# A two-layer cross-attention kernel: the last stage's weight halves are made in the feed-forward and loaded during attention 1

## The reference, cut to what matters

```python
x = x + L0_xattn(layernorm(x), ctx)            # int8 fake-quantised projections
x = x + L0_ffn(layernorm(x))                   # 512 -> 2048 -> 512, gelu of a rounded hidden state
x = x + L1_xattn(layernorm(x), ctx, mask)      # ends as below
x = x + L1_ffn(layernorm(x))

# end of L1_xattn
delta = rs * (ctx_heads @ Wo.T + bo)
delta = (delta - mean(delta)) / sqrt(var(delta) + 1e-5) * gamma + beta

# L1_ffn: a shared two-layer part, and one expert weighted by the softmax over the top 2 gates
logits = x @ W_gate.T
shared = relu(x @ W_up.T) @ W_down.T
out = shared + sum(softmax(top_2(logits))) * (x @ W_expert)
```

## Time and profile before

| what | value |
|---|---|
| three runs: median (lowest to highest) | 2832.75 us (2831.48 to 2833.82) |
| profiled execution: time, and span from first to last instruction | 2833.96 us, 2832.1 us |
| TensorE: matrix products busy | 2595.5 us, 92% of the span |
| VectorE, ScalarE, GpSimd busy | 64%, 44%, 43% |
| mean granted TensorE clock | 0.968 of full speed |
| transfers | 383.83 MB, mean 136 GB/s |
| last stage, 2558 to 2832: TensorE busy | 208.77 of 274.10 us |

### The profile page before, as it was taken

The page is one execution under the profiler, slowest core; times in us unless marked ns, Lnnn a source line. Parts: engine busy times, 40 slices in busy tenths (PEclk is TensorE's granted clock), DMA queues, the critical chain, the costliest instruction groups (busy, mean ns, idle before and its releaser), DMA issues. The chain is left out here.

```text
span 2832.1 us, 35427 instructions
## 1 busy us (share of the span) xinstructions
PE 2595.5 (92%) x14009; PEld 1677.5 (59%) x14024; DVE 1806.8 (64%) x2532; ACT 1249.2 (44%) x1876; POOL 1220.5 (43%) x312
## 2 busy tenths in 40 slices
PE   8999899998999999999958999997999999992998
PEld 7888788985444444445426777775344433432776
DVE  4553444466666766667525755544999999985664
ACT  3221212313656665656632222222888877872211
POOL 1000000004999999999930000000777777772110
PEclk9999999999999999999988999998999999996999
DMA  8676666565534435253044333336977777703110
GB/s 297 205 253 226 221 227 236 188 199 121 104 81 89 97 72 113 62 119 65 16 150 170 112 103 122 110 103 165 197 153 153 154 154 153 154 21 119 61 44 30
DMA packets 206071, 383.83 MB, mean 136 GB/s; under 512 B 16104, under 2 KB 91912, under 8 KB 205840
## 3 DMA queue, kind: packets, MB, share of 16 engines
q1 hardware_dynamic: 205904, 381.56, 49.0%
HBM read 247.92 MB, written 131.94 MB: 134 GB/s over the span
## 5 line engine op out<-in xcount | busy, mean ns | idle before, releaser
L1175 POOL TENSOR_TENSOR pooled<-pooled,probs 128x2048 f32<-128x2048 f32 x140 | 640.3, 4574 | 20.1
L1084 ACT ACTIVATE probs<-psum 128x512 f32<-128x512 f32 (+1 forms) x832 | 459.1, 598 | 355.2 <-PE psum L1010 352.0
L1111 DVE TENSOR_REDUCE win_max<-psum 128x1 f32<-128x802 f32 x480 | 453.9, 988 | 169.2 <-PE psum L975 169.0
L1845 DVE TENSOR_SCALAR probs<-psum,bound 128x1024 f32<-128x1024 f32 (+1 forms) x416 | 508.0, 1278 | 43.6 <-PE psum L1741 43.3
L1800 ACT ACTIVATE probs<-probs 128x1024 f32<-128x1024 f32 (+1 forms) x416 | 440.7, 1059 | 111.9 <-DVE probs L1845 75.3
L1876 POOL TENSOR_TENSOR pooled<-pooled,probs 128x2048 f32<-128x2048 f32 x80 | 368.4, 4605 | 79.5 <-ACT probs L1800 79.5
L1010 PE MATMUL psum<-q_st,k_st 128*128 128x512 f32 (+1 forms) x832 | 336.0, 438 | 37.1 <-ACT den_sb L1096 17.9
L1010 PEld LDWEIGHTS psum<-q_st,k_st 128*128 128x128 f32 (+1 forms) x832 | 148.9, 185 | 259.8 <-ACT probs L1084 176.4
L196 POOL TENSOR_TENSOR r_q<-ve_q,minus_half 128x4 f32<-128x4 f32 x8 | 8.1, 1011 | 681.8 <-DVE ve_q L172 681.8
L975 PE MATMUL psum<-k_st,q_st 96*128 96x402 f32 x960 | 266.6, 359 | 6.3 <-DVE o_sb L1142 5.0
L1741 PE MATMUL psum<-q_st,k_st 128*128 128x512 f32 (+1 forms) x832 | 250.4, 423 | 8.9 <-PEq L137 8.9
(11 more groups left out here) (271 smaller groups left out, 4600.2 us busy)
## 6 DMA issues: line engine op xcount, KB each, us to landing
k_st<-k_hi SPq DMA_DIRECT2D x64, 801.0 KB, 11.8
k_st<-k_lo SPq DMA_DIRECT2D x48, 801.0 KB, 11.5
k_hi<-kt_hi SPq DMA_DIRECT2D x32, 801.0 KB, 4.1
k_lo<-kt_lo SPq DMA_DIRECT2D x32, 801.0 KB, 6.2
v_rows<-v_out SPq DMA_DIRECT2D x96, 256.0 KB
v_st<-v_rows SPq DMA_DIRECT2D x24, 768.0 KB
q_st<-q_hi SPq DMA_DIRECT2D x64, 256.0 KB, 10.4
w<-w_hi_d SPq DMA_DIRECT2D x64, 256.0 KB, 2.6
```

The costliest lines, as they stand in the source:

```text
L1084: A.activation(probs[i % NPROBS][0:rows, j, :], bank(score_banks.where["score", u, t, j])[0:rows, :], ACT.Exp, scale=1.0 / ROOT).then_inc( ...
L1111: V.tensor_reduce(win_max[:, r, j, c:c + 1], window(windows.where["max", u, i])[:, :, 0:MV], AX.XY, ALU.max).then_inc(max_done, 1)
L1175: G.tensor_tensor(pooled[u % 2][:], before[:], probs[tile(u, k) % NPROBS][:], ALU.add).then_inc(pool_added, 1)
L1845: V.tensor_scalar(probs[i % NPROBS][0:rows, half * W:half * W + W, :], window(("score", u, t, half))[0:rows], bound[0:rows, u // NG, t:t + 1],
```

## The change

The last stage's weights wo, wu, wd and we are split in the feed-forward: 16 tiles of 128x512, each loaded to `h_raw`, copied to `h_hi` by ScalarE, subtracted to `h_lo` by VectorE and stored to DRAM (`wf_hi_d`, `wf_lo_d`). A generator `halves` on each of SP, ScalarE and VectorE does one tile every third step; SP issues the load of a tile three steps before it awaits the low half.

Attention 1 has three key and query slots instead of four, allocated outside it, and six buffers of probabilities instead of five. In its last unit SP's program takes the generator `ahead`: batch 0's attention output, the wo halves, bias, gamma, beta, residual rows and the first halves of wu and we are loaded behind the store of unit 13's output, the rest behind the store of unit 14's. The weights go into the slots that units 13 and 14 have used. The last stage keeps its hidden state and operand in the third slot.

In the last stage TensorE does the projections of batches 0 and 1 in a row; `o_cols`, `o_hi` and `o_lo` are double. The gate's weights are loaded in one transfer and split in one operation each. GpSimd makes no halves.

The diff, cut to its core:

```diff
+        wf_hi_d, wf_lo_d = scratch("wf_hi_d", (4, KT, P, D)), scratch("wf_lo_d", (4, KT, P, D))
...
+                h_raw, h_hi, h_lo = sbuf("h_raw1", [P, D]), sbuf("h_hi1", [P, D], F32R), sbuf("h_lo1", [P, D], F32R)
+                halved = [(a[name][k * P:(k + 1) * P, :], wf_hi_d[i, k], wf_lo_d[i, k])
+                          for i, name in enumerate(("wo1_t", "wu_t", "wd_t", "we")) for k in range(KT)]
...
+                    def halves():
+                        for n in range(len(halved)):
+                            for _ in range(3):
+                                yield
+                            A.wait_ge(h_landed, 16 * (n + 1))
+                            if n:
+                                A.wait_ge(h_stored, 32 * n)
+                            A.activation(h_hi[:], h_raw[:], ACT.Copy).then_inc(h_hi_done, 1)
...
+                    def halves():
+                        for n in range(len(halved)):
+                            for _ in range(3):
+                                yield
+                            V.wait_ge(h_hi_done, n + 1)
+                            V.tensor_tensor(h_lo[:], h_raw[:], f32(h_hi[:]), ALU.subtract).then_inc(h_lo_done, 1)
...
                             for side in sides:
                                 next(side, None)
+                            next(beside, None)
...
+                    def halves():
+                        for _ in range(3):
+                            yield
+                        for n, (src, hi, lo) in enumerate(halved):
+                            load(h_raw[:], src, h_landed)
+                            for _ in range(3):
+                                yield
+                            Y.wait_ge(h_lo_done, n + 1)
+                            store(hi, h_hi[:], h_stored)
+                            store(lo, h_lo[:], h_stored)
...
-            n, NQ = 1, 4
+        def attention_1(k_st, q_st, early_v, bound, ahead):
+
+
+            n, NQ, NSLOT = 1, 4, 3
             POOLED = [0, 1, 3, 5, 7, 9, 11]
-            FIRST_SUM, LAG, W, NPROBS, CLOSE = 2, 2, 2, 5, 8
+            FIRST_SUM, LAG, W, NPROBS, CLOSE = 2, 2, 2, 6, 8
...
-                            if u + 1 >= NG:
-                                Y.wait_ge(scored, score(u + 2 - NG, 0, 0))
+                            if u + 1 >= NSLOT:
+                                Y.wait_ge(scored, score(u + 2 - NSLOT, 0, 0))
                             load_kq(u + 1)
+                        if u == UNITS - 1:
+                            Y.wait_ge(scored, score(u - 1, 0, 0))
+                            next(ahead)
                         if u:
                             if u + 1 < UNITS:
                                 Y.wait_ge(summed, u)
                                 load_v(u + 1)
                             Y.wait_ge(o_done, u)
                             store(o_t_1[u - 1], o_sb[:], o_stored)
+                    Y.wait_ge(scored, score(UNITS - 1, 0, 0))
+                    for _ in ahead:
+                        pass
...
+                o_cols = [o_first, sbuf("o1_cols1", [P, KT, S])]
+                o_hi = [sbuf(f"o1_hi{i}", [P, KT, S], F32R) for i in range(2)]
+                o_lo = [sbuf(f"o1_lo{i}", [P, KT, S], F32R) for i in range(2)]
+                delta = sbuf("o1_delta", [P, RT, D])
...
-                        for _ in range(3 + PAUSE):
-                            yield
+                        if b >= 2:
+                            for _ in range(3 + PAUSE):
+                                yield
...
-                    weights.wait_on_pe(NWO)
-                    for _ in projected(0):
+                    M.wait_ge(w_landed["wo"], 32)
+                    for _ in chain(projected(0), projected(1)):
                         pass
                     operand(0)
-                    weights.wait_on_pe(NW)
+                    M.wait_ge(wg_lo_done, 1)
                     for b in range(B):
-                        side = projected(b + 1) if b + 1 < B else iter(())
+                        side = projected(b + 1) if 0 < b < B - 1 else iter(())
...
+                            if b == f == 0:
+                                M.wait_ge(w_landed["wu"], 32)
...
-                    def projected(b):
+                    def low_part(b):
                         yield
                         for g in range(NG):
                             V.wait_ge(o_hi_done, b * NG + g + 1)
...
+                    for _ in chain(low_part(0), low_part(1)):
+                        pass
                     V.wait_ge(rows_given, 64)
                     V.tensor_scalar(rs[:], rs[:], 0.0, 0.3, ALU.max, ALU.min).then_inc(rs_ready, 1)
                     V.wait_ge(rs_ready, 1)
...
+                    V.wait_ge(wg_hi_done, 1)
+                    V.tensor_tensor(wg_lo[:, :, 0:NE], wg_raw[:], f32(wg_hi[:, :, 0:NE]), ALU.subtract).then_inc(wg_lo_done, 1)
+                    for _ in projected(0):
...
-                        advance(side, 2)
+                        advance(side, 2 if b else RT)
...
-                    load_o(0)
-                    for j in range(NWO):
-                        weights.on_sp(j)
-                    load(bo[:], a["bo1"].partition_broadcast(P), rows_given)
+                    load_o(1)
                     load(rs[:], a["rs"].partition_broadcast(P), rows_given)
-                    load_rows(0)
-                    load(gamma[:], a["gamma"].partition_broadcast(P), rows_given)
-                    load(beta[:], a["beta"].partition_broadcast(P), rows_given)
-                    for j in range(NWO, NW):
-                        weights.on_sp(j)
-                    load_o(1)
+                    load(wg_raw[:], a["wg_t"].rearrange("(k p) e -> p k e", p=P), wg_landed)
+                    load_o(2)
                     for b in range(B):
                         if b + 1 < B:
                             Y.wait_ge(copied, (b + 1) * RT)
                             load_rows(b + 1)
-                        if b + 2 < B:
-                            load_o(b + 2)
+                        if b + 3 < B:
+                            load_o(b + 3)
...
+            third = lambda slot, i: slot[:].rearrange("p j t -> p (j t)")[:, i * KT * D:(i + 1) * KT * D].rearrange(
+                "p (k c) -> p k c", c=D)
+            w = [(third(k_st[1], 0), third(k_st[1], 1)), (third(k_st[1], 2), third(k_st[2], 0)),
+                 (third(k_st[2], 1), third(k_st[2], 2)), (q_st[1][:], q_st[2][:])]
+
+            def ahead():
+                def load_half(i, half, sem):
+                    load(w[i][half], (wf_hi_d, wf_lo_d)[half][i].rearrange("k p d -> p k d"), sem)
+
+                for g in range(NG):
+                    load(o_first[:, g, :], o_t_1[g], o_landed[0])
+                load_half(0, 0, w_landed["wo"])
+                load_half(0, 1, w_landed["wo"])
+                load(bo[:], a["bo1"].partition_broadcast(P), rows_given)
+                load(rows[:], rows_of(x_mid, 0), x_landed)
+                load(gamma[:], a["gamma"].partition_broadcast(P), rows_given)
+                load(beta[:], a["beta"].partition_broadcast(P), rows_given)
+                load_half(1, 0, w_landed["wu"])
+                load_half(3, 0, w_landed["we"])
+                yield
+                load_half(1, 1, w_landed["wu"])
+                load_half(3, 1, w_landed["we"])
+                load_half(2, 0, w_landed["wd"])
+                load_half(2, 1, w_landed["wd"])
+
+            attention_1(k_st, q_st, v_view, bound, ahead())
+            spare = [*(third(k_st[0], i) for i in range(3)), q_st[0][:]]
```

107 lines of the change are left out of this document (49 added, 58 removed).

## The result

The changed kernel took **2804.15 us**, the median of four runs (2798.07 to 2805.86); the kernel before took 2832.39 beside it (2831.48 to 2833.82). The ratio is **0.9896, with a 95% interval of 0.9879 to 0.9913**. The forecast was 2799, with a range of 2793 to 2811 and a chance of 0.94 for faster. The profiled execution after took 2802.59, its span 2800.8 (before: 2832.1), at a mean granted clock of 0.974.

What follows compares the result with a forecast made beforehand. TensorE was taken to bound the last stage's steady part, behind a start of loading, projection and norms. 2833.96 - 18.5 - 1.8 - 15.45 + 0.7 + 1.2 gave 2800.1; less 1.2 for the median, 2799 us, range 2793 to 2811.

Steps and rivals of the forecast that it cites:

- Term 1: Last stage's start: with loads and halves ready early, the first product comes sooner, saving 18.5 us.
- Term 2: Last stage, from batch 0's first product to its operand's transposes: less weight and gate splitting on VectorE saves 1.8 us.
- VectorE ahead of its reads: Last stage's start: VectorE's added low halves and small operations before its first read are caught up by the fourth; 0.
- Term 3: Last stage: projection 1 moves from batch 0's loop into TensorE's idle time during the norms, saving 15.45 us.
- bank gate: Last stage: batch 0's gate product waits for VectorE to read projection 1's first block from its bank, costing 0.7 us.
- Is VectorE in time?: Last stage, batch 0: VectorE's hidden low halves, 19.1 us, just meet TensorE's down products; taken as 0, up to 3.2 us.
- Term 4: Feed-forward: of 16 added pairs of halves, two stand ahead of TensorE's waits for VectorE, costing 1.2 us.
- Transfers in attention 1: Attention 1: 11.3 MB of early loads finish 10 us before the last output, costing 0.
- attention 1 as long as before: Attention 1: three key slots instead of four and a sixth probabilities buffer change nothing; 0.
- Rival 1: Feed-forward: all 16 pairs sit on the path and cost 9.8 us, a time of 2803 to 2811; chance 0.17.

Runs made afterwards that it cites:

- halves_only: The kernel before with only the feed-forward's 16 pairs of weight halves made and stored, used by nobody; 2833.7 us, ratio 1.0002.
- pairs_30: The kernel before with 30 unused pairs of weight halves in the feed-forward, one in every second step; 2835.9 us, ratio 1.0013.
- start_edits: Changed kernel with the last stage's memsets behind the low halves, six dummy products ahead of the first, and batch 0's gate product in another bank; 2799.8 us.
- loop_projection: The changed kernel with batch 1's output projection back in batch 0's loop; 2815.6 us, ratio 0.9936.
- again: The changed kernel, unaltered, timed a second time; 2801.4 us, ratio 0.9891.
- combined: Changed kernel with five probabilities buffers, memsets behind the low halves, dummy products, another bank for batch 0's gate product, and GpSimd's beta additions held back; 2792.6 us.
- combined_again: The same program as combined, run a second time; 2793.2 us, ratio 0.9859.
- second_part_late: The changed kernel with wu's and we's low halves and both halves of wd loaded behind the barrier, not in attention 1's last unit; 2800.2 us.
- late_weights: The changed kernel with the halves of wu, we and wd loaded behind the barrier instead of in attention 1; 2801.4 us, ratio 0.9888.

## Why the prediction was right, and where it was off

- **Term 1, the start (-18.5).** Measured 22.41 to 3.70: -18.7, from the same two rows. No run takes the early loads back by themselves.
- **Term 2, the chain to the operand (-1.8).** 34.60 to 34.04: -0.6 in after, and 34.0 to 34.5 in the other kernels with this start. Mis-sized by 1.2, in two steps. One is "TensorE's products of batch 0 take as long as before": the clock came up some 4.4 us into them where it had come up after 2.9, and the fourth read stood 13.3 us behind the first product, not 12.6. That is 0.7, and it moves by itself: with the old start the chain took 34.6, 34.6 and 35.6 us (before, halves_only, pairs_30). The other is the saving behind that read, 0.6 instead of 1.1 (21.37 to 20.73 us): the weight half there had cost 0.5 and the gate halves nothing, since they lay beside other work.
- **VectorE ahead of its reads (0).** Right in its result by a margin that the prediction didn't count: the low halves of batch 1 took 6.6 us, not 2.4, since GpSimd's additions ran beside them. VectorE caught up by the fourth read (it idled 0.63 us ahead of it), as the term said it would. In start_edits, with TensorE sooner, it no longer did.
- **Term 3 (-15.45, bank gate +0.7).** Measured by loop_projection: 14.5 net, against 14.75. The profiles of before and after alone give 14.3 from the transposes to batch 0's store (62.08 to 47.74). The bank gate cost 0.5 to 0.6, not 0.7: 2.06 against 1.50 of wait, and 5.70 against 5.18 from the transposes to the gate product.
- **Is VectorE in time? (0, up to 3.2).** In after, the fourth low half began at 2631.66 and took 0.68, and the down products began at 2634.24: 1.9 us of room. In start_edits it was 0.73 too late. The count of 19.1 against 19.15 was that near. The top-2 operations beside GpSimd's additions took from 1.45 us (again) to 4.31 (start_edits) for the same work.
- **Term 4, the feed-forward (+1.2).** The two waits came at 0.6 each, where they were forecast; stretch B as a whole grew by 0.7, and by 0.2 in halves_only.
- **Transfers in attention 1 (0).** In time by far: the last window with transfers ended at 2544, 14.8 us ahead of the last store. What failed is the step before it, "attention 1 as long as before", with three slots and a sixth buffer at 0. It took 2.9 us more in the profiled execution. 0.7 are its units, of which the sixth buffer makes 0.3. The other 2.3 are the last piece, 27.78 to 30.05, in which the same small products ran at half the clock from 2550.3 on.
- **Why the clock falls there early.** Not settled. The piece was 27.8 to 28.3 us in the three kernels with the old attention 1 and 28.1 to 30.1 in the eleven with the new, so the change may have a part in it. Chance has one: combined and combined_again are the same program and took 28.14 and 29.59. Transfers in the last unit are not needed for it (second_part_late, 29.75) and don't force it (28.14 to 28.43 in three kernels with them).

- **Rival 1** named the times from 2803 to 2811, into which the median of 2804.15 falls, but not for its reason: the pairs cost 1.2 of waiting and not 9.8.

Against the sum of 2800.1 the profiled execution was 2.5 too slow: +2.9 in attention 1, +1.2 in term 2 and +0.8 in stretch A, against -0.5 in stretch B, -1.7 in batch 3 and some tenths. The -1.7 is the clock's and is luck: in before it fell to half early in batch 3 (0.79 and 0.64 in the windows from 2790 to 2796), in after it stayed at 1.00.

## What to carry to other kernels

Work that TensorE does in a full loop can be worth almost its whole time when it goes into a stretch where TensorE waits for VectorE: 48 products, which took 12.6 us and a wait of 2.8, gave 14.5 us here. Of the loads moved ahead, the 6 MB that were first needed some 48 us into the stage brought nothing that shows. An edit that makes one engine faster may only lengthen its wait for the next: in start_edits TensorE's wait for the norms grew by the 2.5 us that it had gained. Where several edits of 1 or 2 us are to be judged and the time varies by 5, give each its own stretch in the trace, between two rows that every version has, and compare there.

## What the runs showed of the hardware

The clock can fall or stay after like waits, and this spreads the times. Batch 3 took 39.0 us in six profiles with the new last stage, 40.3 to 41.6 in three and 43.0 to 43.1 in two. In some, ScalarE's copies stood longer behind the landing of batch 2's output store, and TensorE idled longer ahead of one transpose. First after:

```profile
2758.79 2.19 ACT L2119 ACTIVATE f_residual<-f_rows 128x512 f32<-128x512 f32 x4 [6.61 <-DMA result<-f_residual]
2761.61 0.63 PE L2064 MATMUL psum<-ident,f_logits_t 128*128 128x128 f32 x4 [1.81 <-ACT f_logits_t L2124]
```

Then second_part_late, with one of its windows:

```profile
2756.04 2.19 ACT L2119 ACTIVATE f_residual<-f_rows 128x512 f32<-128x512 f32 x4 [7.89 <-DMA result<-f_residual]
2758.86 1.09 PE L2064 MATMUL psum<-ident,f_logits_t 128*128 128x128 f32 x4 [3.09 <-ACT f_logits_t L2124]
```

```profile
2759.00:2764.00 5.00, 5.00 (x14) 4.03 (x15) 1.70 (x9) 0.20 (x1) 0.00 (x0) 0.50 0.00 0
```

And late_weights, where TensorE idled as long and the clock stayed up:

```profile
2759.96 0.63 PE L2064 MATMUL psum<-ident,f_logits_t 128*128 128x128 f32 x4 [3.12 <-ACT f_logits_t L2124]
2760.60:2763.60 3.00, 3.00 (x14) 2.42 (x14) 1.34 (x9) 0.19 (x1) 0.00 (x0) 1.00 0.00 0
```

The longer wait by itself cost 1.3 us (batch 3: 40.31 in late_weights against 39.03 in after), the fallen clock another 2.7 (43.04 in second_part_late). The length of the wait alone doesn't decide it: with 3.12 us the clock stayed at 1.00, with 3.09 it went to 0.50; and with 1.86 us (combined) it fell as well, to 0.51 in the window below, where with 1.81 (after) it stayed. What decides isn't shown by these runs. The window of combined, from 1.8 us behind the start of its transposes (2746.19):

```profile
2748.00:2751.00 3.00, 3.00 (x8) 2.34 (x7) 0.20 (x2) 0.00 (x0) 0.00 (x0) 0.51 0.00 0
```
